# Seven counted loops of a graph network kernel written out as straight code

## What is computed

```
L0: scores = sum(query[src] * key[dst]) by head (4), softmax over edges of one src,
    alpha * cnt[src]; out = segment_sum(msg[src] * alpha, dst); W1, batch norm, relu, W2
L1: scores = sum(q[dst] * k[src]) by head (8) * scale + edge_attr @ We + be,
    softmax over edges of one dst; agg = segment_sum(probs * v[src], dst) @ Wo + bo
L2: scores = leaky(e_src[src] + e_dst[dst]) (4 heads), softmax over dst with max(., 0);
    out = segment_sum(alpha * h[src], dst)
L3: agg = segment_sum(edge_weight * x[src], dst);
    out = leaky((agg + x) @ W1.T + b1 + (agg * x) @ W2.T + b2)
```

## Time and profile before

| | |
|---|---|
| Time, median of 3 runs | 13592.22 us (13564.79 to 13597.93) |
| Profiled execution | 13595.42 us, its span 13593.7 us |
| Busy share | VectorE 53%, GpSimd 62%, ScalarE 40%, PE 8% |
| Granted TensorE clock over the span | 0.515 |
| Loads, sort, projection for L0, counting of nodes | 0 to 773 us |
| PB, PA, P1, P2, P3 (first gather to end) | 773 to 3631, 3784 to 6059, 6309 to 8624, 8811 to 11094, 11209 to 13455 us |
| Instructions in the built program | 6,037: VectorE 2400, PE 1504, ScalarE 927, GpSimd 808, SyncE 398 |

### The profile page before, as it was taken

The page is one execution under the profiler, slowest core; times in us unless marked ns, Lnnn a source line. Parts: engine busy times, 40 slices in busy tenths (PEclk is TensorE's granted clock), DMA queues, the critical chain, the costliest instruction groups (busy, mean ns, idle before and its releaser), DMA issues.

```text
span 13593.7 us, 54893 instructions
## 1 busy us (share of the span) xinstructions
PE 1025.3 (8%) x4194; PEld 842.8 (6%) x4194; DVE 7244.3 (53%) x7042; ACT 5389.6 (40%) x6052; POOL 8378.7 (62%) x8674
## 2 busy tenths in 40 slices
PE   4012222222100000003000000200000000000001
PEld 3011111111100000001000000100000000000001
DVE  9533434343367777765888888544444443333333
ACT  2233333333245555543666666333333332222221
POOL 0165555555566666664666666566666657777775
PEclk7555555555555555555555555555555555555555
DMA  7444444444355555543556555333333323323322
GB/s 281 176 134 147 156 149 155 151 149 148 123 163 190 191 187 192 190 159 123 194 192 200 192 194 196 97 97 100 97 101 99 97 85 98 94 92 95 94 92 85
DMA packets 791244, 1957.87 MB, mean 144 GB/s; under 512 B 213947, under 2 KB 419603, under 8 KB 790738
## 3 DMA queue, kind: packets, MB, share of 16 engines
q1 hardware_dynamic: 458010, 1136.08, 23.5%
q0 software_dynamic: 333184, 821.25, 21.7%
HBM read 1217.94 MB, written 738.73 MB: 144 GB/s over the span
## 4 chain that ended last, share of the span: by engine, by line
issue 36%; DVE 23%; POOL 14%; DVEq 9%; ACT 7%; another core or an unknown queue 4%; DMA 4%; SPq 3%; PE 1%; ACTq 0%; POOLq 0%
POOL region L1242 13%; DVE work L1397 7%; DVEq L68 4%; DVE work L1330 3%; DVE psB L1298 3%; DVE psR L1390 2%; DMA region<-start_rows_by_src 2%; ACT work L1493 2%; DVE region L617 1%; DVE psR L1334 1%; DVE region L618 1%; ACT work L1415 1%; DVEq L1403 1%; ACT work L1074 1%
## 5 line engine op out<-in xcount | busy, mean ns | idle before, releaser
L1242 POOL DMA_INDIRECT region<-k,ix_s x1612 | 1520.7, 943 | 1125.8 <-DVEq L1322 613.9
L1298 DVE TENSOR_TENSOR_SCAN psB<-psB,work 128x1792 f32<-128x1792 f32 (+1 forms) x496 | 1485.1, 2994 | 1254.1 <-issue 931.5
L1415 ACT COPY work<-region 128x1664 f32<-128x1664 f32 (+1 forms) x496 | 1165.6, 2350 | 2413.3 <-DMA region<-start_rows_by_src 893.0
L1397 DVE TENSOR_TENSOR_SCAN work<-work,psR 128x1792 f32<-128x1792 f32 (+2 forms) x496 | 1971.4, 3975 | 185.2 <-issue 153.6
L1242 POOL DMA_INDIRECT region<-x,ix_s x1612 | 1709.6, 1061 | 559.9 <-issue 522.5
L1242 POOL DMA_INDIRECT region<-kv,ix_s x1612 | 1523.7, 945 | 778.5 <-issue 488.9
L1242 POOL DMA_INDIRECT region<-h,ix_s x1612 | 1520.8, 943 | 749.1 <-issue 479.8
L1242 POOL DMA_INDIRECT region<-qm,ix_s x1612 | 1523.6, 945 | 732.5 <-issue 595.4
L1493 ACT COPY work<-work 128x1664 f32<-128x1664 f32 (+3 forms) x620 | 1573.8, 2538 | 0.0
L1492 ACT COPY psR<-work 128x128 f32<-128x128 f32 (+2 forms) x496 | 190.1, 383 | 2734.5 <-issue 2241.2
L1382 DVE TENSOR_TENSOR psR<-region,psB 128x1664 f32<-128x1664 f32 x124 | 235.1, 1896 | 1476.8 <-DMA region<-x,ix_s 1476.8
(11 more groups left out here) (303 smaller groups left out, 5305.1 us busy)
## 6 DMA issues: line engine op xcount, KB each, us to landing
region<-start_rows_by_dst SPq DMA_DIRECT2D x248, 832.0 KB
state_p<-work SPq DMA_DIRECT2D x124, 936.0 KB
state_p<-work SPq DMA_DIRECT2D x124, 884.0 KB
region<-start_rows_by_src SPq DMA_DIRECT2D x124, 832.0 KB
start_rows_by_dst<-zero_t SPq DMA_DIRECT2D x62, 1664.0 KB
state_pA<-work SPq DMA_DIRECT2D x124, 832.0 KB
state_p<-work SPq DMA_DIRECT2D x124, 832.0 KB
start_rows_by_src<-zero_t SPq DMA_DIRECT2D x1, 59904.0 KB, 163.6
```

What stands on the lines that cost most here:

```text
L1242: g_.indirect_dma_start(rows_s[b][:, k, 0:wd_s], None, q.tabs, bass.IndirectOffsetOnAxis(ap=ix_s[b][:, k:k + 1], axis=0))\
L1298: nc.vector.tensor_tensor_scan(near_ps[:, 0:m], near_ps[:, 0:m], zt[:, 0:m], 0.0, ALU.mult, ALU.add).then_inc(q.s("held"), 1)
L1397: c.do(nc.vector.tensor_tensor_scan(st[:, 0:F * (K + 1)], decay_at(q, b)[:, 0:F * (K + 1)], summed[:, 0:F * (K + 1)], 0.0, ALU.mult, ALU.add))
L1415: nc.scalar.copy(f_by_t(zt, q.HF)[:, :, 1:K + 1].rearrange("p f t -> p t f"), rows_d[b][:, :, :].rearrange("p t w -> p (t w)")[:, 0:K * q. ...
```

## The change

Seven loops with a loop register (`Fori`) become Python loops, so their bodies are written once per turn: `nodes_pool`, `nodes_act`, `payload_pe`, and the pass loops of GpSimd, VectorE, ScalarE and SyncE, the last four for all five passes. With the turn known, each wait has a constant value and can be fastened to the instruction behind it, each address is a constant, and register arithmetic, moves and branches of the loops go. The three loops of `paysort` (L1179, L1194, L1211), which aren't run with these inputs, stay. The built program has 33,936 instructions: VectorE 11471, GpSimd 9555, ScalarE 7813, PE 3207, SyncE 1890.

```diff
@@ nodes_pool
-            with g_.Fori(0, NG) as g:
+            for g in range(NG):
@@ nodes_act
-            with act.Fori(0, NG) as g:
+            for g in range(NG):
@@ payload_pe
-            with pe.Fori(0, NPAY) as c:
+            for c in range(NPAY):
@@ pass_pool
-            with g_.Fori(0, IT // 2) as i:
+            for i in range(IT // 2):
@@ pass_dve
-            with v.Fori(0, IT // 2 - 1) as i:
+            for i in range(IT // 2 - 1):
@@ pass_act
-            with act.Fori(0, IT // 2 - 1) as i:
+            for i in range(IT // 2 - 1):
@@ pass_sp
-            with sp.Fori(0, IT // 2 - peeled) as i:
+            for i in range(IT // 2 - peeled):
```

## The result

The change takes 13,385.3 us (median of 4, 13,379.2 to 13,390.8) beside 13,595.1 for the kernel before: ratio 0.9849, 95% interval 0.9832 to 0.9867. Forecast were 11,850 us, with a range from 11,760 to 13,000. It is 210 us faster, an eighth of what was forecast, and outside the range.

A forecast was written before the change was run, and what follows sets the result against it. Slow phases from the loops were taken to hold five passes 1742 us above their gathers' pace. 13,595 - 731 - 15 - 242 - 275 - 258 - 221 = 11,853, less 3 gives 11,850 us; range 11,760 to 13,000.

The forecast's parts named there:

- Straight code says: to the loops: Straight code between 8720 and 8810 us ran 546 busy instructions evenly, so the slow phases were laid on the loops.
- P3 ... I lay it on the loops that run beside: P3's gathers, 1.10 us in place of 0.94, were said to be stretched by SyncE's and VectorE's loops.
- PA -242: Pass PA: slow phases end with VectorE's 26 rows per pair in place of 54, saving 242 us.
- P2 -258: Pass P2: slow phases end with VectorE's 26 rows per pair in place of 54, saving 258 us.
- P3 -221: Pass P3: gathers no longer stretched once the loops go, saving 221 us; bounds 0 and -221.
- PB -731: Pass PB: SyncE's loads and PE's signal no longer late, gathers bound it, saving 731 us; bounds 0 and -731.
- PB's tail: Last payload store of PB, issued 39 us after the last gather, lags less: -15 us, bounds 0 and -30.
- The floor: Time the gathers alone need per pass, at 1.248 us each: 2010.5 us, and 2086.8 in PB with its key-row gathers.
- P1 -275: Pass P1: VectorE becomes the bound at 32.7 us per pair, so 15 of the 290 us excess stay.
- Fetching, taken as 0: Fetching 33,936 instructions in some 280 packets was taken to cost 0, with 150 us kept in the range.
- Rival B: Phases stay with fewer instructions to hit; PA, P1, P2 reach the floor, P3 and PB don't: 12,820 us; chance 0.22.
- Rival C: No change: register work lies beside waits for other engines; about 13,590 us, or 13,407 if not hidden; chance 0.05.

The follow-up runs named there:

- m4: Small program in place of the layers: five stages of 300 GpSimd transfers (indirect or plain), four beside a VectorE register loop; 2936.8 us clean chip, 3973.4 slow (kernel before 13,649).
- m2: Small program in place of the layers: 800 small transfers each by SyncE and ScalarE, then again beside 300 gathers and 3000 matmuls; SyncE's 1.40 us apart, not 0.47, beside gathers.

## Why the prediction was wrong

**The step that failed** is "Straight code says: to the loops" under "Does the clock-like slowness belong to the loops or to the chip?". The kernel before, with all its loops, runs PA to P3 at 2012 to 2059 us on a clean chip, and the change's straight VectorE code in P2 is stretched to 1.40 us on a slow one. The stretch of the earlier trace rows is straight, but its 48 GpSimd operations in 90 us are indirect DMAs (scatters, L922) at one per 1.9 us, where the passes issue one per 1.25 and are held to 1.40. It is also short: in the kernel before VectorE's first control instruction of over 0.3 us comes 41 to 87 us after the first gather of PA, P1 and P2, the gathers' own stretching only after six pairs of P3, and 209 gathers in m4. So something may have to fill first. Which of the two kept the stretch even, the slack pace or the short time, wasn't tried. Either way the comparison was of unlike company, not of straight code with loops. The counter-evidence named there (in the earlier trace rows the gathers were over) was the right reading: m2 shows SyncE's issues recover the moment they end.

**"P3 ... I lay it on the loops that run beside"**: refuted. P3 before and after have the same 36.4 us per pair. "The first two pairs are still at 1.248" was the start of each pass, before the slow phase; the earlier trace rows have it too.

**PA -242, P2 -258, P3 -221, PB -731**: measured -22, -35, -3, -72 (and PB's tail -13 of -15). The floor itself, 2010.5 and 2086.8 us, was right: the kernel before has it on clean chips. It was the cause that wasn't in the change's reach. On a slow chip the mean pace of a pass is 1.40 us per gather at best, and the earlier trace rows held that already: PA's and P2's mean pairs were 36.4 and 36.6 (2253.0 / 1611 x 26 = 36.4), made of faster and slower ones, and P3's 36.0. Three passes at nearly the same mean, with unequal work, was a sign of a pace set elsewhere. It also gives the change its part: P1, P2 and PA lost what they had above that pace, 129 us together.

**P1 -275**: the bound by VectorE was right in kind and size, 32.7 forecast and 32.63 measured on clean chips, where it is nearly the whole gain (36.8 of 38.5 us). On the slow chip P1 gave 72.

**Fetching, taken as 0** against up to 150: right. With 277 packets, no gap between two gathers of a half is over 0.32 us in the change's two traces of clean chips, and with GpSimd's loop kept the time is the same (11,730 against 11,731). The slow trace has 274 such gaps of up to 0.88 us in PA, P1 and P3, but P3 before has 57 of them too, with its loop.

**Rival B** (the phases stay, fewer instructions to hit) had the right cause, "gathers and DMAs beside them". Its signs came too: P3 at 36.4 us per pair, PB at 44.5. It failed in its arithmetic: it gave PA, P1 and P2 the pace of 1.248 while holding P3 at 1.40. With the pace of P3 before, 2231 us a pass, for all four it would have said 22 + 70 + 38 = 130 us, and something for PB: near 13,450. Its 0.22 was low, and so was its time of 12,820. **Rival C** was near for clean chips (38.5 us gained, 0.3%) by the way it named, with the register work hidden in four passes and bare in one. The Trainium skill's price for a branch ("Advanced Engine Details and Errata", Control Flow Timing, about 108 ns) would have been the better guide than the 702 ns of the row, though it is over twice what the trace shows: on a clean chip the same branch takes 45 ns.

**What stays open.** Whether a slow chip is always slow, or only at times. What it is on a slow chip that lets one update per 0.70 us into the record while indirect gathers run. Each instruction held for two such steps (1.40) fits a start and an end that must be recorded, but was only argued. All times here, timed ones included, carry a record (each has its granted clock), so whether a slow chip is slow without one isn't known either.
The Trainium skill ("NOTIFIC — the notification-queue block", section Interfaces) says that back-pressure from a full internal store of that block can stall an engine; that agrees with a slow start after a filling, and no run here shows the block itself.

## What to carry to other kernels

Where the same instruction takes 0.04 us in one phase and a fixed 0.70 or 1.40 in another, suspect the chip or its record before the code: run the unchanged kernel on a second chip first, and count in the trace something that the program makes a known number of times. Written-out loops save only the register work on the path of the binding engine, here 0.3% from VectorE's and ScalarE's loops of one pass. To cost a cause, compare stretches of the same length and the same company; a mean shared by passes with unequal work points to one pace behind them, even where the waits that show it differ.

## What the runs showed of the hardware that was not expected

- Between Trainium2 chips, the same program differs by 16% (11,768 and 13,649 us) at the same granted clock, 0.514 to 0.518, and with the same 32.5 us for a pass's first pairs.
- On slow chips, while GpSimd issues indirect gathers, the trace gets 1.43 semaphore updates per us. A VectorE register loop is held to steps of 0.70 to 2.1 us from 6 to 11 us after the first gather in m2 and m4 (one turn of m4's takes 5.6 us), SyncE's and ScalarE's issues come 1.40 us apart in m2, and the gathers themselves are held after 117 to 209 of them. Straight code is held as well: VectorE's in P2 of the change. Plain GpSimd transfers do not do it.
- Without indirect gathers the record of the same chip takes up 68 updates per us, about what m2's two streams make (16 per transfer, one transfer each per 0.48 us: 67).
- In the small programs, after every 113 gathers of 128 rows without a wait between them, the next starts 4.2 to 4.5 us after the one before, on both kinds of chip; in the kernel, with a wait every 13, none does. It wasn't followed up.
